# Products for the row maxima of attention scores on 64 rows of TensorE's array, two query tiles at a time

## The chip, the cores and the metric

The kernel runs on one core of a Trainium2 chip. The metric is device time of one execution in microseconds (us). Of the runs of the kernel before, the median counts. A profile is one execution with the hardware profiler on; times inside it are counted from its first instruction.

## The reference

One transformer layer on `x` of 16 sequences x 512 tokens x 256 channels, in float32. After a layer norm two branches run on the same normalised input, and both are added to `x`:

```
q = xn @ Wq.T;  kv_latent = xn @ Wkv_down.T            # 8 heads of 64; latent rank 64
k, v = kv_latent @ Wk_up.T, kv_latent @ Wv_up.T
attn = softmax(q . k / 8);  attention = (attn @ v) @ Wo.T
gate, up = fp4_linear(xn, w_gate), fp4_linear(xn, w_up)    # blocks of 16, values on a 4-bit grid
ffn = fp4_linear(silu(gate) * up, w_down)
out = x + attention + ffn
```

## The kernel before, in words

Weights are folded once at the start, so that a head's query has 64 numbers and the keys are the 64 numbers of the sequence's latent. Precision is kept by limbs: a value is held as a rounded part (`_hi`) and the rest (`_lo`), both of type float32r. `lat` has 128 partitions: 0 to 63 hold the rounded latent, 64 to 127 the rest of it. `q_hi` holds a head's rounded query twice, on partitions 0 to 63 and again on 64 to 127, so one product over 128 partitions gives rounded query times (rounded latent + rest).

The main work is 128 slots, one for each of 16 sequences x 8 heads; 12 lead slots come before, and weight preparation is mixed into them. Each engine has its own program written out slot by slot, in a fixed order, and engines meet at semaphores only. Slots are software pipelined: slot t computes the maxima of head t+2, the transposed scores, the exponentials and most of the weighted sum of head t, the last part of that sum for head t-1, and half a token tile of the feed-forward part. The slots run as 16 written out, 6 turns of a loop of 16, and 16 written out.

The softmax needs each query's maximum over 512 keys ahead of the exponential. `query_scores` (PE, L838) makes the scores for it: for each of four tiles of 128 queries (`qc`), one product of 128 rows x 128 columns of weights with 512 moving columns into one of two PSUM banks, `mx0` and `mx1`. `max_rows` (DVE, L592) takes one bank's maximum along its 512 columns into a column of `row_max`. Tiles 0 and 1 are done early in the slot (after the gate products), tiles 2 and 3 later (after the first two weighted sums for two key tiles). A product for tile `qc` waits until the maximum of tile `qc - 2` has been taken. Then L914 transposes `row_max` into bank `m2`, ACT negates it into `neg_max` (L509), and SP sends it by a DMA into row 64 of `q_lo`.

The order on PE in a slot: gate products (L905), `query_scores` 0 and 1, the transpose of `row_max` of head t+1 (L914), up products (L918, after `m1` is free), `key_scores` 0, three transposes (L862), `weigh` (L890, eight products of 65 columns for each call, type float32) and `key_scores` in turn, `query_scores` 2 and 3, nine down products (L938), `key_scores` 2 and 3, and then, by the slot, query products (L959), output products (L976), transposes (L996, L1002, L1010) and `weigh` 2 and 3. The helper `limbs` gives all of gate, up, down, query, latent and output products the line L760. The order on DVE: SiLU part (L636), `max_rows` 0 and 1, `ht_lo` (L643), `hid` (L648), block scales (L568 to L573), the division (L661, L666), `max_rows` 2 and 3, the sum into `acc` (L683), rounding (L578 to L582), and the low limbs `q_lo` (L710), `xt_lo` (L726), `on_lo` (L731) as they come due.

`m2_free` (L823) makes L914 of slot t wait for what slot t-1 still read from bank `m2`: `xt_lo` after odd slots, `on_lo` or `lat_tok` after even ones. `m1_free` (L812) does so for bank `m1` ahead of the up products. Once for each sequence ACT copies the latent from `m1` (L522, L523) and DVE subtracts for the low half (L704).

In preparation, L788 transposes weight tiles. The gate and up weights have 704 rows, five tiles of 128 and one of 64, and the last tile is loaded as weights on 64 rows:

```
for r in range(0, rows, P):
    m = min(P, rows - r)
    last = pe.transpose(bank[:, r:r + m], w[0:m, a + r // P, k * P:(k + 1) * P], ident[0:m, 0:m])
```

Of the kernel before, what the change touches and what calls it, by code (L numbers as in the profile page):

```python
# [20 lines left out]
ALU = mybir.AluOpType  # L21
ACT = mybir.ActivationFunctionType
AX = mybir.AxisListType
F32 = mybir.dt.float32
# [3 lines left out]
P = 128  # L28
# [41 lines left out]
def transformer_layer(nc, x, Wq, Wkv_down, Wk_up, Wv_up, Wo, w_gate, w_up, w_down, out):  # L70
# [17 lines left out]
    with ExitStack() as ctx:  # L88
        def sb(name, shape, dt=F32):
            return ctx.enter_context(nc.sbuf_tensor(name, shape, dt))  # L90
# [10 lines left out]
        xt_lo = sb("xt_lo", [P, 2, 2 * KD, T], F32R)  # L101
        lat = sb("lat", [P, 2, T], F32R)
        lat1 = sb("lat1", [R + 1, 2, T], F32R)
        lat_tok = sb("lat_tok", [P, 2, CH, R + 2])
        q_hi = sb("q_hi", [P, QH, T], F32R)
        q_lo = sb("q_lo", [R + 1, QH, T], F32R)
# [53 lines left out]
        def psum(name):  # L160
            return ctx.enter_context(nc.psum_tensor(name, [P, 512], F32))

        mx = [psum("mx0"), psum("mx1")]
        st = [psum("st0"), psum("st1")]
        po = psum("po")
        m0, m1, m2 = psum("m0"), psum("m1"), psum("m2")
# [78 lines left out]
        def q_pair(t):  # L245

            m = t.plus(3).over(2)
            return m if t.c % 2 and m.within(B * PAIRS) else None

        def lat_seq(t):  # L250
            s = t.over(H).plus(1)
            return s if t.c % H == 4 and s.within(B) else None
# [225 lines left out]
        @block.scalar  # L478
        def _(act):
            def jobs(numbers):  # L480
                for n in numbers:
                    _, _, rows, cols, hi, _, factor = JOBS[n]
                    act.wait_ge(w_psum, n + 1)
                    act.activation(hi, WBANKS[n % 4][0:rows, 0:cols], ACT.Copy, scale=factor).then_inc(w_hi_done, 1)

            def slot(t):
                def exp(kc):
                    if t.within(SLOTS):
                        act.wait_ge(st_psum, t.n(CH, kc + 1))

                        if t.any(CH, kc + 1 - 2 * CH):
                            act.wait_ge(pv_done, t.n(CH, kc + 1 - 2 * CH))
                        act.activation(probs[:, t.c % 2, kc, :], st[kc % 2][:, :], ACT.Exp).then_inc(exp_done, 1)  # L493

                if t.within(SLOTS):

                    act.wait_ge(gate_psum, t.n(1, 1))

                    if t.any(1, -1):
                        act.wait_ge(h_grid, t.n(1, -1))  # L500
                    act.activation(hid[:, t.c % 2, :], m0[:, 0:HALF], ACT.Tanh, scale=0.5).then_inc(tanh_done, 1)  # L501
                u = t.plus(1)
                if u.within(SLOTS):

                    act.wait_ge(mt_psum, u.n(1, 1))

                    if u.over(2).any(16):
                        act.wait_ge(neg_placed[u.c % 2], u.over(2).n(16))
                    act.activation(neg_max[:, u.c % 2, :], m2[0:CH, 0:P], ACT.Copy, scale=-1.0).then_inc(neg_done, 1)  # L509
                u = t.plus(-2)  # L510
                if u.within(SLOTS):
                    act.wait_ge(ht_psum, u.n(1, 1))
                    act.activation(ht_hi[:, u.c % 2, :, :], m2[:, 0:NB * P].rearrange("p (k q) -> p k q", k=NB),  # L513
                                   ACT.Copy).then_inc(ht_hi_done, 1)
                exp(0)
                exp(1)
                exp(2)
                exp(3)
                s = lat_seq(t)
                if s is not None:  # L520
                    act.wait_ge(lat_psum, s.n(1, 1))
                    act.activation(lat[:, s.c % 2, :], m1[:, :], ACT.Copy).then_inc(lat_hi_done, 1)  # L522
                    act.activation(lat1[0:R, s.c % 2, :], m1[0:R, :], ACT.Copy).then_inc(lat_hi_done, 1)  # L523
                m = q_pair(t)
                if m is not None:

                    act.wait_ge(q_psum, m.n(1, 1))

                    if m.any(2 * CH, -2 * CH):
                        act.wait_ge(st_psum, m.n(2 * CH, -2 * CH))  # L530
                    for u in range(2):
                        for v in range(2):
                            act.activation(q_hi[v * R:(v + 1) * R, 2 * m.c % QH + u, :], m1[u * R:(u + 1) * R, :],  # L533
                                           ACT.Copy).then_inc(q_hi_done, 1)
                n = next_chunk(t)
                if n is not None:
                    c, b = n.c % CH, n.over(CH).c % 2
                    act.wait_ge(xt_psum, n.n(1, 1))
                    act.activation(xt_hi[:, b, :, c * P:(c + 1) * P], m2[:, :].rearrange("p (k q) -> p k q", k=2 * KD),
                                   ACT.Copy).then_inc(xt_hi_done, 1)  # L540
                m = turned_pair(t)
                if m is not None:

                    act.wait_ge(on_psum, m.n(1, 1))

                    if m.over(PAIRS).any(2):
                        act.wait_ge(wov_psum, m.over(PAIRS).n(2))
                    act.activation(on_hi[:, m.c % PAIRS, :], m2[:, :], ACT.Copy).then_inc(on_hi_done, 1)
                s = ltok_seq(t)
                if s is not None:  # L550

                    act.wait_ge(ltok_psum, s.n(1, 1))
                    act.activation(lat_tok[:, s.c % 2, :, 0:R], m2[:, :].rearrange("p (c r) -> p c r", c=CH)[:, :, 0:R],
                                   ACT.Copy).then_inc(ltok_part, 1)

            for t in LEAD:
                jobs(lead_work(t)[1])
                slot(t)
            all_slots(act, slot)

        @block.vector
        def _(dve):
# [26 lines left out]
                        dve.scalar_tensor_tensor(lo, WBANKS[n % 4][0:rows, 0:cols], factor, hi.bitcast(F32),  # L589
                                                 ALU.mult, ALU.subtract).then_inc(w_lo_done, 1)  # L590

            def max_rows(t, qc):  # L592
                u = t.plus(2)
                if u.within(SLOTS):
                    dve.wait_ge(mx_psum, u.n(CH, qc + 1))
                    dve.tensor_reduce(row_max[:, u.c % 2, qc:qc + 1], mx[qc % 2][:, :], AX.X, ALU.max).then_inc(mx_taken, 1)  # L596

            def weight_scales(q):
                w, rows, cols = WQUANT[q]
# [17 lines left out]
            def slot(t):  # L617
# [17 lines left out]
                    dve.wait_ge(tanh_done, t.n(1, 1))  # L635
                    dve.scalar_tensor_tensor(h, h, 1.0, m0[:, 0:HALF], ALU.add, ALU.mult).then_inc(silu_done, 1)  # L636
                max_rows(t, 0)
                max_rows(t, 1)
                u = t.plus(-2)
                if u.within(SLOTS):  # L640

# [14 lines left out]
                if v.within(SLOTS):  # L656
# [7 lines left out]
                    if m.any(1, -1):  # L664
                        dve.wait_ge(on_psum, m.n(1, -1))
                    dve.tensor_tensor(on[:, m.c % 2, :, v.c % 2 * R:(v.c % 2 + 1) * R], heads[:, :, 0:R],  # L666
                                      inv.unsqueeze(2).broadcast_to([P, CH, R]), ALU.mult).then_inc(on_done, 1)
                max_rows(t, 2)
                max_rows(t, 3)
                if u.within(SLOTS):  # L670

                    s, c, j = u.over(H), u.c % H // 2, u.c % 2
# [26 lines left out]
                    to_grid(h_norm[:, :], hid[:, t.c % 2, :], h_round, t)  # L699
                s = lat_seq(t)  # L700
                if s is not None:
                    dve.wait_ge(lat_hi_done, s.n(2, 1))
                    low = lat[R:P, s.c % 2, :]
                    dve.tensor_tensor(low, m1[R:P, :], low.bitcast(F32), ALU.subtract).then_inc(lat_lo_done, 1)  # L704
                m = q_pair(t)
# [49 lines left out]
        def _(pe):  # L755
# [56 lines left out]
            def m1_free(t):  # L812

                if q_pair(t) is not None:
                    pe.wait_ge(q_hi_done, q_pair(t).n(4, 4))
                    pe.wait_ge(q_lo_done, q_pair(t).n(2, 2))
                elif lat_seq(t) is not None:
                    pe.wait_ge(lat_hi_done, lat_seq(t).n(2, 2))
                    pe.wait_ge(lat_lo_done, lat_seq(t).n(1, 1))
                elif t.within(SLOTS):  # L820
                    pe.wait_ge(hid_done, t.n(1, 1))
# [13 lines left out]
                elif t.plus(1).within(SLOTS):  # L835
                    pe.wait_ge(neg_done, t.n(1, 2))

            def query_scores(t, qc):  # L838

                u = t.plus(2)  # L840
                if u.within(SLOTS):
                    s, m = u.over(H), u.over(2)
                    if qc == 0:
                        pe.wait_ge(q_hi_done, m.n(4, 2 * (u.c % 2) + 2))
                        pe.wait_ge(lat_hi_done, s.n(2, 2))
                        pe.wait_ge(lat_lo_done, s.n(1, 1))
                    if u.any(CH, qc - 1):
                        pe.wait_ge(mx_taken, u.n(CH, qc - 1))
                    pe.matmul(mx[qc % 2][:, :], q_hi[:, u.c % QH, qc * P:(qc + 1) * P], lat[:, s.c % 2, :],  # L849
                              start=True, stop=True).then_inc(mx_psum, 1)  # L850

            def turn_hidden(t):
                u = t.plus(-2)
# [41 lines left out]
            def slot(t):  # L895
# [9 lines left out]
                    limbs(m0[:, 0:HALF], [(xt_hi[:, b, KD + k, tok], xt_lo[:, b, KD + k, tok], wgu_hi[:, k, cols],  # L905
                                           wgu_lo[:, k, cols]) for k in range(KD)]).then_inc(gate_psum, 1)
                query_scores(t, 0)
                query_scores(t, 1)
                u = t.plus(1)
                if u.within(SLOTS):  # L910

                    m2_free(t.plus(-1))
                    pe.wait_ge(mx_taken, u.n(CH, CH))
                    pe.transpose(m2[0:CH, 0:P], row_max[:, u.c % 2, :], ident[:, :]).then_inc(mt_psum, 1)  # L914
                if t.within(SLOTS):
                    m1_free(t.plus(-1))
# [5 lines left out]
                weigh(t, 0)  # L922
                key_scores(t, 1)
                weigh(t, 1)
                query_scores(t, 2)
                query_scores(t, 3)
                u = t.plus(-2)
                if u.within(SLOTS):

# [115 lines left out]
```

## Time and profile before

| | |
|---|---|
| median of 3 runs | 1725.3 us (1715.19 to 1727.47) |
| profiled execution | 1716.95 us, its span 1715.2 us |
| PE (products) busy | 1579.9 us, 92% |
| PEld (weight loads) busy | 1440.3 us, 84% |
| DVE busy | 1355.8 us, 79% |
| ACT busy | 695.6 us, 41% |
| POOL busy | 518.2 us, 30% |
| mean granted TensorE clock | 0.977 |

A product's record lasts longer than its hold on the array, since products are pipelined; the step from one start to the next tells what it costs. The chain of waits follows the work that ended last back from the end; in its rows each piece has just the time that it kept the chain.

### The profile page before, as it was taken

Reading aid. Unit: us, or ns where it says so; the run is one execution under the profiler, and the core shown is the slowest. Engines: PE = TensorE matmul, PEld = TensorE weight load, DVE = VectorE, ACT = ScalarE, POOL = GpSimd, SP = SyncE. Lnnn points to the kernel's source line nnn. Section 1 sums busy time; section 2 is a strip of 40 time slices with the busy share of each in tenths; the row PEclk is TensorE's granted clock in tenths of the full one; section 3 lists DMA queues with packets and bytes.
Section 4 is the critical chain, followed back from the end, with each engine's and each line's share of the span. In section 5 each row is a group of like instructions: output and inputs, shape, how many; then the busy total and the mean of one; then the engine's idle time right before and its main releaser. Section 6 shows DMA issues by size and latency. Waiting matters only on the chain.

```text
span 1715.2 us, 33440 instructions
## 1 busy us (share of the span) xinstructions
PE 1579.9 (92%) x10726; PEld 1440.3 (84%) x10726; DVE 1355.8 (79%) x3400; ACT 695.6 (41%) x1350; POOL 518.2 (30%) x696
## 2 busy tenths in 40 slices
PE   0589999999989999999989999899999999999998
PEld 0468898989889898898989899798988989899897
DVE  8788887888877788788778888777887878787763
ACT  0234444444434434444443444344444444344432
POOL 6423322333223233233232323223323223222211
PEclk9789999999999999999999999999999999999999
DMA  3000000000000000000000000000000000000000
GB/s 97 7 7 7 7 17 8 20 8 10 14 9 17 7 20 4 15 14 7 17 9 20 4 14 14 6 20 7 10 14 9 20 4 20 4 14 7 1 14 13
DMA packets 22926, 23.06 MB, mean 13 GB/s; under 512 B 3280, under 2 KB 22224, under 8 KB 22736
## 3 DMA queue, kind: packets, MB, share of 16 engines
q1 hardware_dynamic: 22736, 20.65, 4.0%
q8 instruction: 104, 1.70, 0.4%
q14 instruction: 86, 0.70, 0.1%
HBM read 11.99 MB, written 8.39 MB: 12 GB/s over the span
## 4 chain that ended last, share of the span: by engine, by line
PE 84%; DVE 10%; issue 4%; ACT 1%; DMA 0%; DVEq 0%; POOL 0%; SPq 0%; ACTq 0%; POOLq 0%
PE m L760 34%; PE po L890 22%; PE mx L849 7%; PE st L875 7%; PE st L876 6%; PE m L862 2%; PE m L996 1%; PE m L1002 1%; PE m L914 1%; DVE hid L580 1%; DVE row_max L596 1%; DVE hid L578 1%; DVE on_lo L731 1%; DVE h_small L568 1%; PE m L1010 1%
## 5 line engine op out<-in xcount | busy, mean ns | idle before, releaser
L890 PEld LDWEIGHTS po<-lat_tok,probs 128*128 128x128 f32 x4096 | 519.1, 192 | 22.5
L890 PE MATMUL po<-lat_tok,probs 128*128 128x65 f32 x4096 | 514.9, 269 | 0.0
L493 ACT ACTIVATE probs<-st 128x512 f32<-128x512 f32 x512 | 291.4, 595 | 341.2 <-PE st L876 341.2
L596 DVE TENSOR_REDUCE row_max<-mx 128x1 f32<-128x512 f32 x512 | 327.6, 681 | 0.6 <-PE mx L849 0.6
L410 POOL TENSOR_TENSOR h_norm<-hid,h_small 128x352 f32<-128x352 f32 x128 | 100.9, 788 | 469.2 <-DVE h_small L573 469.2
L875 PE MATMUL st<-q_hi,lat 128*128 128x512 f32 x512 | 213.9, 418 | 0.0
L876 PE MATMUL st<-q_lo,lat 65*128 65x512 f32 x512 | 204.4, 399 | 0.0
L760 PE MATMUL m<-wgu_hi,xt_hi 128*128 128x352 f32 x512 | 191.8, 375 | 8.9 <-issue 8.7
L710 DVE TENSOR_TENSOR q_lo<-m,q_hi 64x512 fp32r<-64x512 f32 x128 | 88.0, 688 | 122.9 <-ACT q_hi L533 122.9
L441 POOL TENSOR_TENSOR h_norm<-h_norm,hid 128x352 f32<-128x352 f32 x128 | 119.6, 934 | 216.3 <-DVE h_norm L582 216.3
L849 PE MATMUL mx<-lat,q_hi 128*128 128x512 f32 x512 | 177.1, 428 | 3.6 <-DVE row_max L596 3.5
L533 ACT ACTIVATE q_hi<-m 64x512 fp32r<-64x512 f32 x256 | 151.4, 591 | 61.7 <-PE m L760 57.0
L760 PE MATMUL m<-wgu_lo,xt_hi 128*128 128x352 f32 x512 | 169.1, 330 | 0.0
L760 PE MATMUL m<-wgu_hi,xt_lo 128*128 128x352 f32 x512 | 168.5, 329 | 0.0
L513 ACT ACTIVATE ht_hi<-m 128x384 fp32r<-128x384 f32 x128 | 62.7, 490 | 199.7 <-PE m L862 199.7
L643 DVE TENSOR_TENSOR ht_lo<-m,ht_hi 128x384 fp32r<-128x384 f32 x128 | 71.2, 556 | 68.1 <-ACT ht_hi L513 68.0
L760 PEld LDWEIGHTS m<-wgu_hi,xt_hi 128*128 128x128 f32 x512 | 100.0, 195 | 27.5 <-issue 16.2
L501 ACT ACTIVATE hid<-m 128x352 f32<-128x352 f32 x128 | 59.4, 464 | 128.2 <-PE m L760 125.5
L760 PE MATMUL m<-wd_hi,ht_hi 128*128 128x256 f32 x384 | 107.6, 280 | 1.3 <-DVE ht_lo L643 1.3
L760 PE MATMUL m<-wd_hi,ht_lo 128*128 128x256 f32 x384 | 107.3, 280 | 0.0
L760 PE MATMUL m<-wd_lo,ht_hi 128*128 128x256 f32 x384 | 107.2, 279 | 0.0
L410 POOL TENSOR_TENSOR hq<-h_norm,h_small 128x352 f32<-128x352 f32 x128 | 100.7, 787 | 10.0
(175 smaller groups left out, 3054.0 us busy)
## 6 DMA issues: line engine op xcount, KB each, us to landing
x_in<-in_L_attn_x_dram SPq DMA_DIRECT2D x64, 128.0 KB, 2.1
out_dram<-acc SPq DMA_DIRECT2D x32, 256.0 KB, 2.2
q_lo<-neg_max SPq DMA_DIRECT2D x128, 2.0 KB
weights_in<-in_L_ffn_w_down_dram SPq DMA_DIRECT2D x1, 704.0 KB, 6.4
weights_in<-in_L_ffn_w_gate_dram SPq DMA_DIRECT2D x1, 640.0 KB, 4.7
acc<-in_L_ffn_w_up_dram SPq DMA_DIRECT2D x1, 640.0 KB, 5.9
wq_in<-in_L_attn_Wq_dram SPq DMA_DIRECT2D x1, 512.0 KB, 6.1
x_in<-in_L_attn_Wo_dram SPq DMA_DIRECT2D x1, 512.0 KB, 7.0
```

The costliest lines, as they stand in the source:

```text
L410: return pool.tensor_tensor(blocks(dst), blocks(src), per_block.unsqueeze(2).broadcast_to([rows, cols // BLOCK, BLOCK]), ALU.mult)
L441: pool.tensor_tensor(h_norm[:, :], h_norm[:, :], hid[:, w.c % 2, :], ALU.subtract).then_inc(h_grid, 1)
L493: act.activation(probs[:, t.c % 2, kc, :], st[kc % 2][:, :], ACT.Exp).then_inc(exp_done, 1)
L533: act.activation(q_hi[v * R:(v + 1) * R, 2 * m.c % QH + u, :], m1[u * R:(u + 1) * R, :], ACT.Copy).then_inc(q_hi_done, 1)
L596: dve.tensor_reduce(row_max[:, u.c % 2, qc:qc + 1], mx[qc % 2][:, :], AX.X, ALU.max).then_inc(mx_taken, 1)
L643: dve.tensor_tensor(ht_lo[:, u.c % 2, :, :], m2[:, 0:NB * P].rearrange("p (k q) -> p k q", k=NB), ht_hi[:, u.c % 2, :, :].bitcast(F32), AL ...
L710: dve.tensor_tensor(q_lo[0:R, h, :], m1[v * R:(v + 1) * R, :], q_hi[v * R:(v + 1) * R, h, :].bitcast(F32), ALU.subtract).then_inc(q_lo_don ...
L760: last = pe.matmul(dst, a, b, start=(n == 0), stop=(n == len(ms) - 1))
L849: pe.matmul(mx[qc % 2][:, :], q_hi[:, u.c % QH, qc * P:(qc + 1) * P], lat[:, s.c % 2, :], start=True, stop=True).then_inc(mx_psum, 1)
L875: pe.matmul(st[kc % 2][:, :], lat[:, s.c % 2, keys], q_hi[:, h, :], start=True, stop=False)
L876: pe.matmul(st[kc % 2][:, :], lat1[:, s.c % 2, keys], q_lo[:, h, :], start=False, stop=True).then_inc(st_psum, 1)
L890: last = pe.matmul(po[:, qc * P:qc * P + R + 1], probs[:, u.c % 2, kc, qc * P:(qc + 1) * P], lat_tok[:, s.c % 2, kc, 0:R + 1], start=(kc = ...
```

## The change

`mx` becomes one PSUM tensor of two banks. For each half of the query tiles (0 and 1, then 2 and 3) two products are made, each over 64 partitions: the first tile's with `q_hi` and `lat` on partitions 0 to 63 into the first bank, the second tile's with `q_hi` on 64 to 127 and a new tile `lat_up` into the second bank. `lat_up` is the rounded latent on partitions 64 to 127, written by one more ACT copy for each sequence. The maxima are so taken of rounded query times rounded latent, without the latent's rest. One DVE instruction takes both banks' maxima (1024 columns into two). The semaphores follow: one count for a pair of products and one for a pair of maxima; a pair of products waits for the maximum over the pair before; DVE's subtraction L704 and the users of the latent wait for three ACT copies in place of one or two.

```
-        mx = [psum("mx0"), psum("mx1")]
+        mx = ctx.enter_context(nc.psum_tensor("mx", [P, 2, 512], F32))
...
+                    act.activation(lat_up[R:P, s.c % 2, :], m1[R:P, :], ACT.Copy).then_inc(lat_hi_done, 1)
...
-                    dve.wait_ge(mx_psum, u.n(CH, qc + 1))
-                    dve.tensor_reduce(row_max[:, u.c % 2, qc:qc + 1], mx[qc % 2][:, :], AX.X, ALU.max).then_inc(mx_taken, 1)
+                    dve.wait_ge(mx_psum, u.n(2, half + 1))
+                    dve.tensor_reduce(row_max[:, u.c % 2, 2 * half:2 * half + 2], mx[:, :, :], AX.X, ALU.max).then_inc(mx_taken, 1)
...
                 max_rows(t, 0)
-                max_rows(t, 1)
...
-                max_rows(t, 2)
-                max_rows(t, 3)
+                max_rows(t, 1)
...
-                    dve.wait_ge(lat_hi_done, s.n(2, 1))
+                    dve.wait_ge(lat_hi_done, s.n(3, 3))
...
-                    if u.any(CH, qc - 1):
-                        pe.wait_ge(mx_taken, u.n(CH, qc - 1))
-                    pe.matmul(mx[qc % 2][:, :], q_hi[:, u.c % QH, qc * P:(qc + 1) * P], lat[:, s.c % 2, :],
-                              start=True, stop=True).then_inc(mx_psum, 1)
+                    if u.any(2, half):
+                        pe.wait_ge(mx_taken, u.n(2, half))
+                    a, b = slice(2 * half * P, (2 * half + 1) * P), slice((2 * half + 1) * P, (2 * half + 2) * P)
+                    pe.matmul(mx[:, 0, :], q_hi[0:R, h, a], lat[0:R, s.c % 2, :], start=True, stop=True)
+                    pe.matmul(mx[:, 1, :], q_hi[R:P, h, b], lat_up[R:P, s.c % 2, :], start=True, stop=True).then_inc(mx_psum, 1)
...
                 query_scores(t, 0)
-                query_scores(t, 1)
...
-                    pe.wait_ge(mx_taken, u.n(CH, CH))
+                    pe.wait_ge(mx_taken, u.n(2, 2))
...
-                query_scores(t, 2)
-                query_scores(t, 3)
+                query_scores(t, 1)
```

## Rows read from the trace of the kernel before

**Rows 1.** The page, its parts on busy time and on 40 slices.

```profile
PE 1579.9 (92%) x10726; PEld 1440.3 (84%) x10726; DVE 1355.8 (79%) x3400; ACT 695.6 (41%) x1350; POOL 518.2 (30%) x696
...
PEclk9789999999999999999999999999999999999999
```

**Rows 2.** The page, its part on the chain that ended last.

```profile
PE 84%; DVE 10%; issue 4%; ACT 1%; DMA 0%; DVEq 0%; POOL 0%; SPq 0%; ACTq 0%; POOLq 0%
PE m L760 34%; PE po L890 22%; PE mx L849 7%; PE st L875 7%; PE st L876 6%; PE m L862 2%; PE m L996 1%; PE m L1002 1%; PE m L914 1%; DVE hid L580 1%; DVE row_max L596 1%; DVE hid L578 1%; DVE on_lo L731 1%; DVE h_small L568 1%; PE m L1010 1%
```

**Rows 3.** Busy time by stretch: PE, PEld, DVE, ACT, POOL, granted clock, DMA.

```profile
67.00:68.10 1.10, 1.10 (x9) 0.74 (x7) 1.06 (x3) 1.10 (x3) 0.00 (x0) 1.00 0.69 192
...
100.00:500.00 400.00, 381.82 (x2617) 347.93 (x2616) 327.87 (x820) 175.15 (x339) 121.30 (x161) 1.00 0.04 11
```

**Rows 4.** The chain of waits, 820 to 829: start, us, what.

```profile
822.90 0.46 PE mx L849 x2
...
825.22 0.84 PE po L890 x8
...
827.43 0.53 PE mx L849 x2
...
828.98 0.23 PE st L875
```

**Rows 5.** Timeline of PEld, 66.8 to 68.2: start, us, what, [idle before].

```profile
66.66 0.14 PEld L788 LDWEIGHTS m<-ident,weights_in 128*128 128x128 f32 x1
66.77 0.58 PEld L788 LDWEIGHTS st<-ident,weights_in 128*128 128x128 f32 x5
67.52 0.14 PEld L788 LDWEIGHTS st<-ident,weights_in 64*128 64x128 f32 x1 [0.17 <-issue]
67.72 0.39 PEld L788 LDWEIGHTS po<-ident,weights_in 128*128 128x128 f32 x2
```

**Rows 6.** Groups by line: busy us, mean ns, idle before.

```profile
L596 DVE TENSOR_REDUCE row_max<-mx 128x1 f32<-128x512 f32 x512 | 327.6, 681 | 0.6 <-PE mx L849 0.6
...
L876 PE MATMUL st<-q_lo,lat 65*128 65x512 f32 x512 | 204.4, 399 | 0.0
...
L568 DVE TENSOR_REDUCE h_small<-hid 128x22 f32<-128x352 f32 x128 | 66.6, 520 | 4.5
```

**Rows 7.** Who waited for whom, 115 to 1676: total us, times, longest.

```profile
PEld m L914 <- ACT xt_hi L539: 26.8, 32, 0.8
PE m L914 <- issue: 16.7, 39, 0.4
...
PEld mx L849 <- DVE row_max L596: 0.8, 2, 0.4
```

**Rows 8.** Timeline of all engines, 846.85 to 848.7.

```profile
846.89 0.60 ACT L539 ACTIVATE xt_hi<-m 128x512 fp32r<-128x512 f32 x1
...
847.36 0.63 PE L849 MATMUL mx<-lat,q_hi 128*128 128x512 f32 x2
...
847.62 0.69 DVE L726 TENSOR_TENSOR xt_lo<-m,xt_hi 128x512 fp32r<-128x512 f32 x1
...
848.39 0.08 PEld L914 LDWEIGHTS m<-ident,row_max 128*4 128x4 f32 x1 [0.83 <-ACT xt_hi L539]
```

**Rows 9.** Timeline of DVE and PE around the tightest maxima, 810.8 to 813.

```profile
810.85 1.28 DVE L596 TENSOR_REDUCE row_max<-mx 128x1 f32<-128x512 f32 x2
...
812.75 0.48 PE L849 MATMUL mx<-lat,q_hi 128*128 128x512 f32 x1
```

**Rows 10.** Timeline of ACT, DVE and PE around the latent, 451 to 455.

```profile
451.67 0.58 ACT L523 ACTIVATE lat<-m 64x512 fp32r<-64x512 f32 x1
...
452.49 0.69 DVE L704 TENSOR_TENSOR lat<-m,lat 64x512 fp32r<-64x512 f32 x1
453.22 0.69 DVE L731 TENSOR_TENSOR on_lo<-m,on_hi 128x512 fp32r<-128x512 f32 x1
...
454.57 0.27 PE L914 MATMUL m<-ident,row_max 128*4 128x128 f32 x1
```

More of the change, by code:

```diff
@@ L103, in transformer_layer @@
         lat1 = sb("lat1", [R + 1, 2, T], F32R)
+        lat_up = sb("lat_up", [P, 2, T], F32R)
         lat_tok = sb("lat_tok", [P, 2, CH, R + 2])
@@ L590, in jobs, with max_rows @@
                                                  ALU.mult, ALU.subtract).then_inc(w_lo_done, 1)
-            def max_rows(t, qc):
+            def max_rows(t, half):
                 u = t.plus(2)
                 if u.within(SLOTS):
-                    dve.wait_ge(mx_psum, u.n(CH, qc + 1))
-                    dve.tensor_reduce(row_max[:, u.c % 2, qc:qc + 1], mx[qc % 2][:, :], AX.X, ALU.max).then_inc(mx_taken, 1)
+                    dve.wait_ge(mx_psum, u.n(2, half + 1))
+                    dve.tensor_reduce(row_max[:, u.c % 2, 2 * half:2 * half + 2], mx[:, :, :], AX.X, ALU.max).then_inc(mx_taken, 1)
             def weight_scales(q):
@@ L817, in m1_free @@
                 elif lat_seq(t) is not None:
-                    pe.wait_ge(lat_hi_done, lat_seq(t).n(2, 2))
+                    pe.wait_ge(lat_hi_done, lat_seq(t).n(3, 3))
                     pe.wait_ge(lat_lo_done, lat_seq(t).n(1, 1))
@@ L836, in m2_free, with query_scores @@
                     pe.wait_ge(neg_done, t.n(1, 2))
-            def query_scores(t, qc):
+            def query_scores(t, half):
                 u = t.plus(2)
                 if u.within(SLOTS):
-                    s, m = u.over(H), u.over(2)
-                    if qc == 0:
+                    s, m, h = u.over(H), u.over(2), u.c % QH
+                    if half == 0:
                         pe.wait_ge(q_hi_done, m.n(4, 2 * (u.c % 2) + 2))
-                        pe.wait_ge(lat_hi_done, s.n(2, 2))
+                        pe.wait_ge(lat_hi_done, s.n(3, 3))
                         pe.wait_ge(lat_lo_done, s.n(1, 1))
-                    if u.any(CH, qc - 1):
-                        pe.wait_ge(mx_taken, u.n(CH, qc - 1))
-                    pe.matmul(mx[qc % 2][:, :], q_hi[:, u.c % QH, qc * P:(qc + 1) * P], lat[:, s.c % 2, :],
-                              start=True, stop=True).then_inc(mx_psum, 1)
+                    if u.any(2, half):
[3 more added lines that the diff above has]
+                    pe.matmul(mx[:, 1, :], q_hi[R:P, h, b], lat_up[R:P, s.c % 2, :], start=True, stop=True).then_inc(mx_psum, 1)
             def turn_hidden(t):
```

## The prediction

> **What bounds the kernel now.** I read the busy times first: PE 92%, its weight loads 84%, DVE 79% [rows 1]. A busy PE alone proves little, since its records overlap, so the chain of waits comes next: 84% of it is PE, and the products for the maxima (L849) are 7% [rows 2]. In a stretch of the steady part PE is busy 382 of 400 us at full granted clock [rows 3]. So PE's stream of products is the bound, and what shortens or lengthens it there shows in the end time, except in slots where PE already stands still.
>
> What the products for the maxima cost is read from the chain, not from their mean record. The early pair of a slot keeps the chain 0.46 us, two times 0.23; the late pair, which follows the eight `weigh` products, keeps it 0.53 [rows 4]. Another 512-column product, L875, costs 0.23 too [rows 4], though it works on 128 rows; L876, on 65 rows, has about the same record [rows 6]. The time goes by moving columns, not by rows. So halving the rows of a product saves nothing by itself: a gain can only come from two products of 64 rows that run side by side.
>
> Where PE stands still: L914 waits for bank `m2`. In 39 slots of the steady part it starts late [rows 7]. One is seen whole: DVE's `xt_lo` ends at 848.31, and the load for L914 comes at 848.39, after 0.83 us without a load, while the pair of products had begun at 847.36 and holds the array 0.46 us [rows 8]. `xt_lo` follows ACT's `xt_hi`, and both hang on transposes that lie ahead of the gate products. So whatever the early pair gains or loses in these 39 slots goes into this wait. In the other 89 slots the early pair is on the path, and the late pair is in all 128. That makes 217 pairs on the path, of 256.
>
> **What the change does on PE.** The trace of before has no 64-row float32r product, but it has weights on 64 rows: the last tile of the gate and up weights, four times in preparation. The loads of the 128-row tiles in front come 0.11 us apart: five in 0.58 us with the last one's own 0.14. The fifth so starts at 67.21 and the next would be due at 67.32. The 64-row load starts at 67.52, after 0.17 us of idle time that no semaphore explains [rows 5]; the granted clock is full there [rows 3]. The product in front runs from 67.32 to 67.43; then 0.09 us pass in which the array is emptied before the load may come. Then the 128-row load behind it starts at 67.72, 0.20 us after the 64-row load, though that product has 64 columns only (half of 0.11): 0.15 over. The load after that (again on 64 rows) starts at 67.72 + 0.39 - 0.14 = 67.97, that is 0.25 us on, of which 0.11 is the product: 0.14 over. I read it so: each change between 128-row and 64-row weights costs 0.09 us in which the array runs empty, and 0.06 us more in the product behind it, whose weights could not be loaded under the product in front.
>
> L876, on 65 rows, shows no idle time in front of its 512 products [rows 6]: not every odd shape pays, the change to 64 rows does.
>
> The Trainium skill states the same as a rule (page TensorEngine Tiling (Array Packing), section Tiling Modes, Key Properties): changing the tiling mode, not merely the tile, drains TensorE, while different tiles load and multiply in parallel. The trace agrees with the first half; no row bears on the second.
>
> A pair of 64-row products stands alone between 128-row work, so it pays the change twice. Step by step, from the end of the product in front to the point where the next product's weights are in: 0.09 empty; 0.06 for the first load; 0.11 until the second half's load is in too, since loads never come closer than 0.11 [rows 5]; 0.23 for the second product, the first running beside it; 0.09 empty; 0.06 for the next load. Sum 0.64, rounded down to 0.63 because 0.23 contains a small gap of its own. Against 0.46 that is +0.17 for an early pair. The late pair costs 0.53 now, since behind float32 products the first load already shows; +0.10 to +0.11 there.
>
> Sum: 89 early pairs x 0.17 = 15 us, 128 late pairs x 0.11 = 14 us, together +29 us.
>
> The Trainium skill would have the two products start about 4 ns apart (page TensorE: Matmul & The Clock Gate, Part 3, Measured speedup vs the span model). By it the 0.11 of the second load falls away, and the sum would be +5 us. The page's packs run many of their kind in a row; no row here shows a pair.
>
> **The bounds of that.** Below: if both loads lie in the time in which the array empties, the sum loses 217 x 0.11 = 24 us, to +5. Above: if the two products do not overlap at all, the second adds 0.22 in place of 0.11, +24 us, to +53. I take the middle because loads at 0.11 are what the rows show, and because the two products share neither rows nor bank.
>
> **What the change does elsewhere.** DVE: a maximum over 512 columns takes 681 ns, over 352 columns 520 [rows 6]; 1 ns for a column, so 1024 columns take some 1.20 us, where the two now take 1.28 together [rows 9]. That is 0.08 x 256 = 20 us of DVE's time. It buys nothing: DVE is idle for 2.8 us of each slot, and the wait of L914 hangs on ACT and DVE work that starts from PE's own products [rows 8]. DVE must now wait for both products of a pair; it comes to them late, and has waited for a product only 0.6 us in the whole run [rows 6]. At nothing, then; if that cover went, 0.1 us for each.
>
> PE gets a longer wait: the late pair now needs the maxima of both early tiles where the first of its products needed one. In the tightest of the eight kinds of slot the pair of maxima ends at 812.13 and the late product starts at 812.75 [rows 9]: 0.62 us to spare. In the timeline of the other kinds it is over 1.6 in nearly all slots. So nothing is added. Today's wait on the maxima is 0.8 us in total [rows 7]. If DVE fell behind by more than 0.6 us, all of PE's slot would queue behind this wait.
>
> ACT and the latent, 16 times: one more copy of 0.58 us, started 0.48 after the one in front. L704 needs all three now: the third ends near 452.73 instead of a start at 452.49, so L704 and `on_lo` behind it move by 0.3 us, `on_lo` to 454.2. L914 comes at 454.57 [rows 10]. 0.3 us of cover is left; nothing is added. Were it gone, 15 x 0.3 = 5 us. SP, POOL and the DMAs are not touched, nor is the order of anything else.
>
> **From the profile to the forecast.** The profiled execution took 1716.95 us; with +29 it is 1746. It lies 8 us below the median of the runs, 1725.3; the same +29 gives 1754 there, 1.7% more. Within 1% is about what a measurement of this kernel can't tell from no change, so 17 us.
>
> **Rivals.**
> 1. *Faster: side by side and no emptying between float32r products.* Then the pair's loads hide under the product in front, and the second product lags by one load: 0.23 + 0.11 = 0.34 against 0.46, 217 x 0.12 = 26 us less, 1699. With both loads early the pair would cost 0.23, 217 x 0.23 = 50 us less, 1675. For it: the four 64-row loads seen belong to float32 transposes in preparation, and none to a plain product. Against it: the gap lies at exactly these loads, at full clock and without a semaphore. It decides from the point where the two changes of mode cost less than the 0.12 won for a pair, 0.06 each; they were read at 0.15. Chance 0.19.
> 2. *Changes are paid and the two products run one after the other.* +53 us, 1778. For it: the two share the 128 columns on which results leave the array, and no row shows an overlap of products. Against it: different rows, different banks. Chance 0.20.
> 3. *Changes are paid, loads hidden in them*: +5 us, 1730. Chance 0.13.
> 4. *The change does not do what it says on the array*: the products run in the 128-row arrangement as L876 does. Then all stays: 1725, less than 5 us either way. Chance 0.06.
>
> The forecast itself, changes paid and the second product one load behind, has 0.42; its own range is 1740 to 1765, and a tenth of it falls under 1%.
>
> **How the numbers follow.** Slower by over 1%: 0.38 of the forecast and rival 2, 0.58. Within 1%: 0.04, rival 3 and rival 4, 0.23. Faster: 0.19. The range reaches from rival 1's nearer value, with a few us for the scatter of the runs (1715 to 1727), to rival 2's: 1695 to 1785.
>
> **What would show it.** In the profile after, the chain's piece for an early pair should be near 0.63 us instead of 0.46, for a late one near 0.63 instead of 0.53; the weight load of the first 64-row product should have some 0.1 to 0.2 us of idle time before it that no semaphore explains, and the 128-row load behind the pair again. The starts of the two products should lie 0.11 us apart; 0.23 would be rival 2, and loads under the product in front with no idle time rival 1. Waits of L914 after odd slots should shrink by 0.17 us each. DVE busy should fall by 20 us with no use to the end time. The forecast is wrong if float32r products with 64 rows change mode for free, if the loads of the two halves overlap, or if DVE, now one instruction for two tiles, comes late for the late pair in more than the tightest kind of slot.

## The result and the profile after

The changed kernel takes 1738.3 us (median of 6 runs, 1733.8 to 1748.5) against 1725.0 before; the ratio is 1.0084 (95% interval 1.0048 to 1.012). It is slower, as forecast, but by 0.8% where 1.7% was forecast. The profiled executions are 1733.8 and 1716.95 us, 17 us apart.

The page of the kernel after, its parts on busy time, slices and the chain, answers to [rows 1, 2]:

```profile
PE 1597.7 (92%) x10726; PEld 1402.9 (81%) x10726; DVE 1334.6 (77%) x3144; ACT 705.4 (41%) x1366; POOL 519.2 (30%) x696
...
PEclk9789999999999999999999999999999999999999
...
PE 86%; DVE 9%; issue 4%; ACT 1%; DMA 0%; POOL 0%; DVEq 0%; SPq 0%; POOLq 0%
```

PE is busy 18 us more and DVE 21 us less, and the end came later: DVE's saving bought nothing. The single maximum takes 1.22 us, and a product of 64 rows has a longer record (513 ns) than one of 128 rows had. Three groups by line of the kernel after:

```profile
L598 DVE TENSOR_REDUCE row_max<-mx 128x2 f32<-128x1024 f32 x256 | 311.3, 1216 | 1.8 <-PE mx L851 1.8
...
L850 PE MATMUL mx<-lat,q_hi 64*128 64x512 f32 x256 | 131.3, 513 | 5.6 <-DVE row_max L598 5.6
...
L851 PE MATMUL mx<-lat_up,q_hi 64*128 64x512 f32 x256 | 131.4, 513 | 0.0
```

The timeline of weight loads around one early pair shows what happens on the array:

```profile
835.31 0.18 PEld L850 LDWEIGHTS mx<-lat,q_hi 64*128 64x128 f32 x1 [0.22 <-issue]
835.31 0.18 PEld L851 LDWEIGHTS mx<-lat_up,q_hi 64*128 64x128 f32 x1
835.74 0.08 PEld L914 LDWEIGHTS m<-ident,row_max 128*4 128x4 f32 x1 [0.25 <-issue]
```

and the timeline of loads around the late pair of the same slot:

```profile
839.90 0.18 PEld L850 LDWEIGHTS mx<-lat,q_hi 64*128 64x128 f32 x1
839.90 0.18 PEld L851 LDWEIGHTS mx<-lat_up,q_hi 64*128 64x128 f32 x1
840.33 0.19 PEld L760 LDWEIGHTS m<-wd_hi,ht_hi 128*128 128x128 f32 x1 [0.25 <-issue]
```

Three things are to be seen. The two loads of a pair come at the same moment, not 0.11 us apart. There is idle time that no semaphore explains: before the load of an early pair (0.22 us) and before the load behind either pair (0.25), but not before a late pair, which follows the float32 products. And a pair holds the array 0.43 us from its loads to the next load, though each product streams for 0.23 only. The products themselves (timeline of PE, after):

```profile
835.31 0.50 PE L850 MATMUL mx<-lat,q_hi 64*128 64x512 f32 x1
835.31 0.50 PE L851 MATMUL mx<-lat_up,q_hi 64*128 64x512 f32 x1
835.74 0.27 PE L914 MATMUL m<-ident,row_max 128*4 128x128 f32 x1
```

The chain of waits after, 820 to 850 (start, us, what), answers to [rows 4]:

```profile
835.38 0.43 PE mx L850
835.81 0.00 PE mx L851
835.81 0.20 PE m L914
...
839.97 0.42 PE mx L850
840.39 0.01 PE mx L851
840.40 1.26 PE m L760 x9
```

L850 keeps the chain for the whole pair and L851 for nothing: they run side by side. But the pair's 0.43 stands against 0.46 and 0.53 before, and the cost is pushed to its neighbours. The same neighbours in the chain of the kernel before, two pieces of 820 to 829 and one from behind it:

```profile
823.36 0.11 PE m L914
...
827.96 1.02 PE m L760 x9
...
840.99 1.06 PE m L760 x9
```

L914 is 0.20 instead of 0.11, the nine down products 1.26 instead of 1.02 to 1.06. From the start of the product in front to the second start behind (medians over some 120 slots of the timeline): an early pair takes 0.715 us, 0.654 before (+0.06); a late pair 0.857, 0.746 before (+0.11).

Waits for other engines did not grow (who waited for whom, after, 115 to 1690), beside [rows 7]:

```profile
DVE lat L704 <- ACT lat_up L525: 10.1, 15, 2.2
...
PE m L914 <- issue: 18.2, 39, 0.5
...
PEld mx L850 <- DVE row_max L598: 0.6, 1, 0.6
```

In as many slots as before, 39, the product L914 starts late. That the early pair hides there can be read from its start: in the three of the eight kinds of slot that wait in nearly every sequence, L914 starts 1.21 to 1.22 us after the last gate product in both kernels (medians); in the other five it starts 0.61 to 0.63 us after it before and 0.68 to 0.69 after. By these starts more slots wait than 39: 51 before and 52 after.

The late pair's longer wait on the maxima cost 0.6 us in the steady part. In the first slots, ahead of 115 us, it cost more: over the whole run PE waits 5.6 us for L598 at L850, as the group above has it, where it waited 3.5 us at L849 before. DVE's longer wait for the latent has no one waiting for it. One other wait took up a part of the loss: PE stands still for `on_lo` ahead of the token transposes (L1010 before, L1009 after) for 31.5 us before and 28.8 after.

### The profile page after: what moved, and what is told of

Read it like the earlier page. It is cut to its first block, busy times and chain, and to the rows that moved or that the text cites. A ratio compares the mean times of both kernels' runs of the same rounds, so it can differ in the third digit from the quotient of the medians.

```text
span 1732.0 us, 33242 instructions
## 1 busy us (share of the span) xinstructions
PE 1597.7 (92%) x10726; PEld 1402.9 (81%) x10726; DVE 1334.6 (77%) x3144; ACT 705.4 (41%) x1366; POOL 519.2 (30%) x696
## 4 chain that ended last, share of the span: by engine, by line
PE 86%; DVE 9%; issue 4%; ACT 1%; DMA 0%; POOL 0%; DVEq 0%; SPq 0%; POOLq 0%
PE m L760 36%; PE po L891 23%; PE st L876 7%; PE st L877 6%; PE mx L850 6%; PE m L863 2%; PE m L914 2%; PE m L995 1%; PE m L1001 1%; DVE hid L582 1%; DVE row_max L598 1%; DVE hid L580 1%; DVE h_small L570 1%; DVE on_lo L731 1%; PE m L1009 1%
## 5 line engine op out<-in xcount | busy, mean ns | idle before, releaser
L598 DVE TENSOR_REDUCE row_max<-mx 128x2 f32<-128x1024 f32 x256 | 311.3, 1216 | 1.8 <-PE mx L851 1.8
L850 PE MATMUL mx<-lat,q_hi 64*128 64x512 f32 x256 | 131.3, 513 | 5.6 <-DVE row_max L598 5.6
L851 PE MATMUL mx<-lat_up,q_hi 64*128 64x512 f32 x256 | 131.4, 513 | 0.0
L760 PE MATMUL m<-wd_hi,ht_hi 128*128 128x256 f32 x384 | 120.7, 314 | 1.3 <-DVE ht_lo L644 1.3
```

What stands on the lines that cost most here:

```text
L598: dve.tensor_reduce(row_max[:, u.c % 2, 2 * half:2 * half + 2], mx[:, :, :], AX.X, ALU.max).then_inc(mx_taken, 1)
L760: last = pe.matmul(dst, a, b, start=(n == 0), stop=(n == len(ms) - 1))
L850: pe.matmul(mx[:, 0, :], q_hi[0:R, h, a], lat[0:R, s.c % 2, :], start=True, stop=True)
L851: pe.matmul(mx[:, 1, :], q_hi[R:P, h, b], lat_up[R:P, s.c % 2, :], start=True, stop=True).then_inc(mx_psum, 1)
```

## The experiments

All times are medians, ratios are to the kernel before on the same chip.

**All of the change but its rows** (both products of a pair on 128 rows again).

```
-                    pe.matmul(mx[:, 0, :], q_hi[0:R, h, a], lat[0:R, s.c % 2, :], start=True, stop=True)
-                    pe.matmul(mx[:, 1, :], q_hi[R:P, h, b], lat_up[R:P, s.c % 2, :], start=True, stop=True).then_inc(mx_psum, 1)
+                    pe.matmul(mx[:, 0, :], q_hi[:, h, a], lat[:, s.c % 2, :], start=True, stop=True)
+                    pe.matmul(mx[:, 1, :], q_hi[:, h, b], lat[:, s.c % 2, :], start=True, stop=True).then_inc(mx_psum, 1)
```

> All of the change but its rows: both products of a pair work on 128 rows as before, with one maximum over both banks, the extra copy and the longer waits. Theory (the loss is the change of mode on PE): 1725 us, within 5 of before. Rival (the loss comes from the single maximum, the late pair waiting for it, or the later low half of the latent): 1738 as the changed kernel. In the profile the theory wants the early pair to keep the chain 0.46 us again and the late one 0.53.

Measured: 1731.9 us, ratio 1.0033 (1.0015 to 1.0051), 12 runs. Its chain of waits:

```profile
837.30 0.23 PE mx L850
837.53 0.23 PE mx L851
837.76 0.11 PE m L914
```

The pair keeps 0.46 us again and L914 its 0.11; the late one has 0.28 and 0.23, as before. The rows are what changed PE's stream. Yet some 6 us remain. They aren't on PE's stream: in the timeline the kinds of slot without a long idle stretch have the lengths of before to 0.05 us, most of them to 0.01. They lie in the granted clock. Its mean over a run is 0.966 (median of 12 runs) against 0.972 (20 runs of before). In each sequence PE stands still for some 2.1 us ahead of L1010 (L1009 here), waiting for `on_lo`; behind it the clock often falls to its lower level. Two places of the kernel before, and then one of this kernel (columns as in [rows 3]):

```profile
577.00:581.00 4.00, 1.88 (x18) 1.65 (x18) 3.06 (x9) 1.16 (x4) 1.86 (x3) 1.00 0.00 0
581.00:584.50 3.50, 3.50 (x15) 3.40 (x15) 1.34 (x4) 0.66 (x2) 1.83 (x3) 0.51 0.00 0
679.00:682.00 3.00, 0.82 (x9) 0.68 (x7) 2.20 (x5) 0.60 (x1) 1.80 (x3) 1.00 0.00 0
682.00:686.00 4.00, 4.00 (x28) 3.66 (x28) 2.98 (x7) 1.11 (x3) 1.91 (x3) 1.00 0.00 0
```

```profile
690.50:692.00 1.50, 0.05 (x1) 0.05 (x1) 1.36 (x3) 0.02 (x1) 0.67 (x2) 0.88 0.00 0
692.00:698.50 6.50, 6.50 (x25) 6.10 (x26) 2.77 (x6) 1.12 (x3) 2.45 (x4) 0.50 0.00 0
```

Before, the clock is at 1.2 GHz for some 3.5 us behind the first idle stretch and doesn't fall at all behind the second; here it is at 1.2 GHz for 6.5 us behind one as long. Both kernels have short and long falls. Between 115 and 1690 us the profiled execution of before has 9 of them, 37.5 us in all, and this one 14, 75 us in all. At half the clock that is 19 us more, and 18 lie between the two executions (1735.2 and 1716.95). So a difference of some 6 us between two of these kernels can be clock alone, and from here on I give the mean clock beside the time. Why one kernel has more and longer falls than the other isn't shown. Neither the theory's "within 5" nor the rival's 1738 was met; the chain sides with the theory.

**Two maxima in place of one.**

```
-                    dve.tensor_reduce(row_max[:, u.c % 2, 2 * half:2 * half + 2], mx[:, :, :], AX.X, ALU.max).then_inc(mx_taken, 1)
+                    dve.tensor_reduce(row_max[:, u.c % 2, 2 * half:2 * half + 1], mx[:, 0, :], AX.X, ALU.max)
+                    dve.tensor_reduce(row_max[:, u.c % 2, 2 * half + 1:2 * half + 2], mx[:, 1, :], AX.X, ALU.max).then_inc(mx_taken, 1)
```

> The changed kernel with two maxima of 512 columns in place of one of 1024. Theory: DVE is busy for some 20 us more, in time that it has to spare, so 1738 us, within 5. Rival (DVE's share is on the path): 1738 + 10 to 20, so the single maximum hides part of PE's loss.

Measured: 1738.1 us, ratio 1.0094 (1.0068 to 1.0119), clock 0.972, and DVE busy 1350.4 us against 1334.6. DVE's saving lies in time that it has to spare.

**Both products of a pair on the same 64 rows.**

```
-                    pe.matmul(mx[:, 1, :], q_hi[R:P, h, b], lat_up[R:P, s.c % 2, :], start=True, stop=True).then_inc(mx_psum, 1)
+                    pe.matmul(mx[:, 1, :], q_hi[0:R, h, b], lat[0:R, s.c % 2, :], start=True, stop=True).then_inc(mx_psum, 1)
```

> Both products of a pair on partitions 0 to 63, so they cannot run side by side, while the mode stays that of 64 rows. Theory (records 0.004 us apart mean that the two really run together): each pair is longer by a product of 0.21 to 0.23 us; late pairs 128 x 0.22 = 28, early ones 89 x 0.22 = 20, so 1738 + 48 = 1786 us. Rival (their records only look parallel, and the 0.43 us of a pair already hold two streams): 1738, unchanged.

Measured: 1789.2 us, ratio 1.0371 (1.0342 to 1.0401). The timeline of PE and then of loads around a late pair:

```profile
849.50 0.49 PE L850 MATMUL mx<-lat,q_hi 64*128 64x512 f32 x1
849.84 0.39 PE L851 MATMUL mx<-lat,q_hi 64*128 64x512 f32 x1
```

```profile
849.50 0.18 PEld L850 LDWEIGHTS mx<-lat,q_hi 64*128 64x128 f32 x1
849.61 0.19 PEld L851 LDWEIGHTS mx<-lat,q_hi 64*128 64x128 f32 x1
```

On the same rows the second load comes 0.11 us later and the second product 0.34 later, 0.23 of stream behind an open load of 0.11. A pair is longer by 0.23 us than one on different rows. So the overlap is real, it is worth 51 us in this kernel, and the loads overlap too when the rows differ.

**Only the early, and only the late pair on 64 rows** (the other half with the two 128-row products of the first experiment; the late-only kernel has the test turned round).

```
+                    if half == 0:
+                        pe.matmul(mx[:, 0, :], q_hi[0:R, h, a], lat[0:R, s.c % 2, :], start=True, stop=True)
+                        pe.matmul(mx[:, 1, :], q_hi[R:P, h, b], lat_up[R:P, s.c % 2, :], start=True, stop=True).then_inc(mx_psum, 1)
+                    else:
+                        pe.matmul(mx[:, 0, :], q_hi[:, h, a], lat[:, s.c % 2, :], start=True, stop=True)
+                        pe.matmul(mx[:, 1, :], q_hi[:, h, b], lat[:, s.c % 2, :], start=True, stop=True).then_inc(mx_psum, 1)
```

> Only the early pair on 64 rows, the late one on 128. In the traces an early pair costs 0.06 us more than on 128 rows, and 39 of the 128 stand ahead of a wait that takes it up: 89 x 0.06 = 5 us over the kernel with both pairs on 128 rows and all else changed (1732), so 1737; and with the late pair's 0.11 x 128 = 14 the two should make up the changed kernel's loss on PE. Rival (both kinds cost the same): 8 us over 1732. Steps of the pair's starts as in the changed kernel: 0.253, 0.003, 0.43.

> Only the late pair on 64 rows, the early one on 128 as before. From the traces a late pair costs 0.116 us more than before, in all 128 slots: 15 us over before, 1740. If both pairs of a slot lose the same, 7: 1732. What is left of the changed kernel's loss is the early pair's, 0.055 us in some 89 slots by the traces, 5 us.

Measured, early only: 1729.6 us, ratio 1.0032 (1.0004 to 1.0059), clock 0.970. Late only: 1733.5 us, 1.0054 (1.0037 to 1.0072), clock 0.973. The forecast times, 1737 and 1740, were not met. As times these stand within the clock's share of each other and of the first experiment (1731.9 at 0.966), so alone they don't settle the split. The steps do: early only has 0.714 and 0.746 us around the pairs, late only 0.655 and 0.856, the same to 0.001 as the changed kernel and the kernel before have for each. If each time is multiplied by its mean clock, for what it would be with no time lost at the lower level, then against both pairs on 128 rows the early pair adds 3 us, the late one 12, both together 15.

**The late pair's products issued twice**, on 64 rows and, in another kernel, on 128 rows.

```
+                    if half == 1:
+                        pe.matmul(mx[:, 0, :], q_hi[0:R, h, a], lat[0:R, s.c % 2, :], start=True, stop=True)
+                        pe.matmul(mx[:, 1, :], q_hi[R:P, h, b], lat_up[R:P, s.c % 2, :], start=True, stop=True)
                     pe.matmul(mx[:, 0, :], q_hi[0:R, h, a], lat[0:R, s.c % 2, :], start=True, stop=True)
                     pe.matmul(mx[:, 1, :], q_hi[R:P, h, b], lat_up[R:P, s.c % 2, :], start=True, stop=True).then_inc(mx_psum, 1)
```

> The changed kernel with the late pair's two products issued twice, into the same banks (work that adds nothing, to price a pair inside a stay in the 64-row arrangement). Theory (entering and leaving is paid once, and inside the stay a pair of streams costs 0.22 us with its loads hidden): 1738 + 128 x 0.22 = 1766 us. Rival (loads of 64 rows are never hidden, or each pair drains): 0.43 us each, 1738 + 55 = 1793.

> The changed kernel with the late half alone altered: its two products on 128 rows, issued twice; the early pair is on 128 rows too where it is issued once more, as in the changed kernel's place, on 64 rows. So against the kernel with only the early pair on 64 rows this adds 128 x 0.46 = 59 us: 1730 + 59 = 1789. Theory: slower than the doubled 64-row pair by some 20 us, so that the arrangement pays from four products in one stay. Rival (0.43 each in the stay): no faster than this one.

The second text is wrong about its kernel: the kernel as run had its early pair on 128 rows, once. It is to be compared with the first experiment, from which the same theory would give 1732 + 59 = 1791. Measured: 1791.0 us on 64 rows (ratio 1.0394, 1.0354 to 1.0435, clock 0.962) and 1800.9 on 128 rows (1.0451, 1.041 to 1.0491, clock 0.964). The timeline of the doubled 64-row pair:

```profile
847.58 0.50 PE L851 MATMUL mx<-lat,q_hi 64*128 64x512 f32 x1
847.58 0.50 PE L852 MATMUL mx<-lat_up,q_hi 64*128 64x512 f32 x1
847.91 0.39 PE L853 MATMUL mx<-lat,q_hi 64*128 64x512 f32 x1
847.92 0.39 PE L854 MATMUL mx<-lat_up,q_hi 64*128 64x512 f32 x1
848.23 0.39 PE L760 MATMUL m<-wd_hi,ht_hi 128*128 128x256 f32 x1
```

The first pair takes 0.33 us to the second, and the second with the emptying behind it 0.32. In the medians the second pair adds 0.233 us; on 128 rows two more products add 0.467. So the change of mode is paid once for a stay. With four products in the late stay 64 rows win 0.12 us there and lose 0.06 at the early pair: 128 x 0.06 = 8 us, and 10 were measured between the two kernels. As a time, 1791.0 is the rival's 1793 and not the theory's 1766; only the steps tell them apart. 64 rows added 53 us in time and 128 x 0.233 = 30 by the steps; the clock, 0.962 against 0.972, is 18 us of the rest.

**The late pair ahead of the second weighted sum.**

```
                 key_scores(t, 1)
+                query_scores(t, 1)
                 weigh(t, 1)
-                query_scores(t, 1)
```

> The changed kernel with the late pair moved ahead of the second weighted sum, so that it is entered from a float32r product and left into float32 ones. Theory (entering behind a float32r product costs 0.087 us over a hidden load, behind float32 products only 0.035; leaving costs an open load of 0.107 either way): 128 x 0.05 = 7 us slower than the changed kernel, 1745. Rival (where the pair stands makes no difference): 1738.

Measured: 1771.3 us, ratio 1.0266 (1.0229 to 1.0303), clock 0.961. Neither was right. On the array the entry costs the same in both places: the pair's loads come 0.330 us after the start of a 512-column product that takes 0.235, and 0.205 after a float32 one that takes 0.112, 0.09 over each. My reason for a dearer entry was wrong. But the pair now comes 0.84 us earlier in most slots, more than the 0.62 us of cover that the tightest kind of slot had, and waits for DVE there (who waited for whom):

```profile
PEld mx L850 <- DVE row_max L598: 10.7, 18, 1.7
```

These 11 us and the lower clock (0.961 for 0.972, up to 19 us) make up most of the 33. It shows how thin the cover of the new wait was.

**The transpose of the row maxima behind the late pair.** The late pair leaves into a load of 128 columns, the early one into L914's load of 4. Moving L914 exchanges them, and takes L914 away from its wait for bank `m2`. Once with the products of before, once with the change:

```
                 query_scores(t, 0)
-                u = t.plus(1)
-                if u.within(SLOTS):
-
-                    m2_free(t.plus(-1))
-                    pe.wait_ge(mx_taken, u.n(2, 2))
-                    pe.transpose(m2[0:CH, 0:P], row_max[:, u.c % 2, :], ident[:, :]).then_inc(mt_psum, 1)
...
                 query_scores(t, 1)
+                u = t.plus(1)
+                if u.within(SLOTS):
+                    if t.plus(-2).within(SLOTS):
+                        pe.wait_ge(ht_hi_done, t.n(1, -1))
+                        pe.wait_ge(ht_lo_done, t.n(1, -1))
+                    else:
+                        m2_free(t.plus(-1))
+                    pe.wait_ge(mx_taken, u.n(2, 2))
+                    pe.transpose(m2[0:CH, 0:P], row_max[:, u.c % 2, :], ident[:, :]).then_inc(mt_psum, 1)
```

ACT's negation moves from ahead of `ht_hi` to behind the second exponential. The transposes L863 wait for bank `m2` as L914 did, and what writes `m2` later in the slot waits for `neg_max`.

> The kernel before, with the transpose of the row maxima (L914) and ACT's negation moved from behind the early products to behind the late ones of the same slot; its wait for bank m2 is then taken by the three transposes behind the first transposed scores. Theory (the wait of L914 for the low limb is 0.7 us in 39 slots and nothing else is late just behind it): 27 us less than before, 1698. Rival (the up products or the first transposed scores are next in line, waiting for the low limb of the query): half of it or less, 1712 to 1725.

> The changed kernel with the same move. Theory: the late pair now leaves into the small weight load of the transpose, so the open load of 0.11 us moves from behind the late pair to behind the early pair; both pairs together cost 0.17 to 0.18 us more than on 128 rows, and no early pair hides in a wait: 128 x 0.17 = 22 us over the same move on the kernel before, 1720. Rival (with the wait gone the change of mode costs less than it gains): no more than 10 us over it.

Measured: on the kernel before 1698.4 us, ratio 0.9845 (0.9808 to 0.9882), clock 0.972; on the changed kernel 1716.5 us, 0.9959 (0.9936 to 0.9983), clock 0.968. The waits at L914 are gone, and little of them came back behind it (PE's wait for `on_lo` is 34.2 us instead of 31.5): 25 us less than before. The chain of the first and then of the second kernel:

```profile
832.09 0.46 PE mx L849 x2
832.54 0.96 PE m L760 x6
...
836.51 0.52 PE mx L849 x2
837.03 0.11 PE m L927
```

```profile
836.91 0.42 PE mx L850
837.33 0.00 PE mx L851
837.33 1.16 PE m L760 x6
...
828.29 0.42 PE mx L850
828.71 0.01 PE mx L851
828.72 0.20 PE m L926
```

The early pair now makes the six products behind it 1.16 us instead of 0.96; the late pair only makes its transpose 0.20 instead of 0.11, and is itself 0.10 shorter. In the medians the early pair costs 0.947 against 0.784 (+0.16), the late one 0.659 against 0.660 (nothing). 128 x 0.16 = 21 us; 18 measured. The nearness of the two is in part luck: 4 us of the 21 go into PE's wait for `on_lo` (34.2 and 30.2 us), and the clock was lower in the second kernel. Each time multiplied by its mean clock, the difference is 11 us, so the rival's "no more than 10" is excluded by the chain and the medians, and not by the time.

**Only that late pair on 64 rows, in the new order.**

> The changed kernel with the transpose of the row maxima behind the late pair, and only that late pair on 64 rows; the early pair is on 128 rows again. Theory (the loss of a pair is the weight load of 128 columns that is open behind it; with the transpose's load of 4 columns there the pair costs what two products on 128 rows cost, 0.66 against 0.66 us): 1698 us, within 5 of the same move on the kernel before. Rival (the loss belongs to the late pair wherever it leaves to, 0.11 us each): 1698 + 14 = 1712.

Measured: 1695.4 us, ratio 0.9834 (0.9802 to 0.9865), clock 0.970. Its chain:

```profile
832.06 0.42 PE mx L851
832.48 0.00 PE mx L852
832.48 0.20 PE m L930
```

The rival's 1712 is out. What the late pair loses is the weight load that is open behind it; with a load of 4 columns there it breaks even. That holds for a pair behind the float32 products, where two products on 128 rows take 0.53 us as well. The early pair of the changed kernel had the same small load behind it and lost 0.06 us, since on 128 rows it takes only 0.46. This is the fastest kernel of the study, but its gain is the moved transpose's: it isn't told apart from 1698.

## Why the prediction was right in its direction and wrong in its size

- *PE's stream is the bound, and rows don't matter to a product's time*: right. PE's share of the chain rose from 84% to 86%, and 256 pairs on 128 rows have the steps of before.
- *Changing to 64-row weights empties the array*: right, and at the forecast price of 0.09 us for each change, though it was read from four transposes in preparation [rows 5].
- *The two products run side by side*: right. It was the assumption with the least behind it, and the same-rows kernel, 51 us slower than the changed one, shows it.
- *The second half's load comes 0.11 us after the first*: this step failed. The loads came 0.003 us apart; 0.11 is the distance of loads on the same rows (seen in the same-rows kernel). In the sum this term is 217 x 0.11 = 24 us that aren't there. The Trainium skill's figure of about 4 ns between tiles (TensorE: Matmul & The Clock Gate, Part 3, Measured speedup vs the span model) holds here for float32r on 64 rows.
- *0.06 for each load that can't hide*: this failed too. It is too small for a load of 128 columns, which takes 0.11, both ahead of a pair (+11 us over 217 pairs) and behind a late one (+6), and too large for the load behind an early one (-5). The right sum for a pair is 0.09 + 0.11 + 0.23 + 0.09 = 0.52 us, and 0.11 more if a load of 128 columns comes behind. That is 0.63 for the late pair, as forecast, by two errors of one size. For the early pair I had not seen that L914's load of 4 columns stands behind it: 0.52 and not 0.63, +0.06 us instead of +0.17. The sum becomes 89 x 0.06 + 128 x 0.11 = 19 us, where 29 were forecast and 17 lie between the profiled executions. So the size was missed in the early pair: the two errors cancelled in the late one.
- *39 early pairs hide in L914's wait, and all late pairs are on the path*: the first is right in kind. The starts of L914 show the early pair hidden wherever it waits, in some 51 slots rather than 39; at 0.06 us a pair the difference is under 1 us. The forecast 0.17 us less of wait for each is 0.06. The second is not quite so: PE's wait for `on_lo` shrank by 3 us.
- *DVE's 20 us buy nothing; the new wait and the latent's extra copy cost nothing*: right in the main, by two maxima in place of one, by 0.6 us of wait in the steady part, and by L704's longer wait that holds up no one. The first slots, ahead of 115 us, were not looked at: there the new wait cost 2 us.
- *The time follows at the median as in the profile*: only to some us. The mean clock moves from run to run (0.965 to 0.979 in the runs of the kernel before), and the kernel with only the rows put back had 0.006 less clock and 6 us more, with the same stream. Between 19 us by the steps and the 13 between the medians, 3 us are the wait for `on_lo`; the rest stays open, and the clock alone can be as much. Why idle stretches of equal length are followed by no fall of the clock, by some 3.5 us at 1.2 GHz or by 6.5 isn't settled either.

## What to carry to other kernels

Products on half the rows run side by side, loads and all, but a stay in that arrangement costs the emptying of the array at both ends and a load that can't hide at each, unless the load behind is small. So count what a stay holds: one pair of 512 columns lost 0.06 to 0.16 us for most stays here, and two pairs in one stay won 0.12. A lone pair broke even in one place only, behind float32 products and with a small weight load behind it. When an instruction shrinks an engine that waits anyway, ask first for the wait on the bound engine: moving one transpose out of a wait gave 1.5% where the whole change of the products lost 0.8%.

## What the runs showed of the hardware that I had not expected

- Two weight loads on different 64-row halves start 0.003 us apart and take 0.18 us each in the records; on the same half they start 0.11 apart.
- The cost of a change of mode shows in the neighbour's record, not in the product's: a pair kept the chain for 0.43 us, less than the 0.46 of before, and the pieces behind it grew by 0.09 and 0.20.
- One idle stretch of PE of 2.1 us per sequence can be followed by a fall of the granted clock to 1.2 GHz, for 3.5 us in one place and 6.5 in another, and it can be followed by none. The mean clock of a kernel moved with changes that had left PE's stream alone (0.972 to 0.966).
